# A decoder layer on one core: another order of the steps, the end in two halves, and the cross stage's maxima added by VectorE

## The reference

```python
x = layernorm(x + attention(x))               # 16 heads of 8, causal, rope before the second projection
x = layernorm(x + cross_attention(x, ctx))    # 16 heads of 8, 154 context tokens, rope, biases
x = layernorm(x + ffn(x))

def ffn(x):                                   # x: 1024 tokens of 128
    probs = softmax(x @ wg.T)                 # 8 experts
    topk_w, topk_idx = top_k(probs, 2)        # renormalised to sum 1
    expert_w = one_hot(topk_idx) summed with topk_w
    h1 = einsum('th,eih->tei', x, w1)         # inner width 256 per expert
    h3 = einsum('th,eih->tei', x, w3)
    y = einsum('tei,ehi->teh', silu(h1) * h3, w2)
    return einsum('te,teh->th', expert_w, y)
```

## Time and profile before

| | |
|---|---|
| median of three runs | 267.58 us (266.43 to 268.08) |
| profiled execution | 266.47 us |
| span of that execution, first to last instruction | 264.7 us |
| mean granted TensorE clock | 0.987 |
| busy share: PE, PEld, DVE, ACT, POOL | 88%, 60%, 69%, 59%, 36% |

### The profile page before, as it was taken

The page is one execution under the profiler, slowest core; times in us unless marked ns, Lnnn a source line. Parts: engine busy times, 40 slices in busy tenths (PEclk is TensorE's granted clock), DMA queues, the critical chain, the costliest instruction groups (busy, mean ns, idle before and its releaser), DMA issues. The chain is left out here.

```text
span 264.7 us, 4496 instructions
## 1 busy us (share of the span) xinstructions
PE 233.1 (88%) x1385; PEld 160.1 (60%) x1385; DVE 184.0 (69%) x614; ACT 156.9 (59%) x311; POOL 95.4 (36%) x153
## 2 busy tenths in 40 slices
PE   7677999989998989999998966979799999999960
PEld 3254775666674656666654344554389788897850
DVE  6558878884999886765955569993177873679543
ACT  1669576786789956875887642547466755221300
POOL 9983292174413355241744511065000102711001
PEclk9979999999999999999999999999999999999997
DMA  6970000001000400000031200001411121101001
GB/s 240 340 264 1 2 0 1 2 29 53 2 0 0 158 2 1 4 0 0 5 115 41 83 0 1 0 30 52 120 30 32 31 62 40 50 22 40 1 1 42
DMA packets 10552, 12.57 MB, mean 47 GB/s; under 512 B 1184, under 2 KB 7712, under 8 KB 10400
## 3 DMA queue, kind: packets, MB, share of 16 engines
q1 hardware_dynamic: 9440, 10.43, 12.1%
q0 software_dynamic: 512, 1.05, 1.3%
q10 hardware_dynamic: 576, 0.79, 0.8%
HBM read 9.25 MB, written 3.01 MB: 46 GB/s over the span
## 5 line engine op out<-in xcount | busy, mean ns | idle before, releaser
L1450 DVE CUSTOM_DVE_ANT_0 junk<-psA,c 128x128 bf16<-128x128 f32 (+3 forms) x128 | 56.0, 487 | 14.2 <-PE psA L969 13.6
L1244 ACT ACTIVATE prob<-psB 128x512 f32<-128x512 f32 (+1 forms) x88 | 47.1, 559 | 13.2 <-PE psB L998 12.5
L969 PE MATMUL psA<-kst,qa 128*128 128x512 f32 (+1 forms) x88 | 37.7, 441 | 3.7 <-DVE negm L1450 1.8
L998 PE MATMUL psB<-qb,kst 128*128 128x512 f32 (+3 forms) x128 | 38.6, 346 | 2.5 <-ACT prob L1244 1.0
L998 PEld LDWEIGHTS psB<-qb,kst 128*128 128x128 f32 x128 | 22.8, 188 | 17.8 <-issue 8.5
L1455 DVE TENSOR_REDUCE negm<-psA 128x3 f32<-128x462 f32 (+1 forms) x48 | 26.3, 578 | 10.1 <-PE psA L969 10.0
L1244 ACT ACTIVATE prob_more<-psB 128x512 f32<-128x512 f32 (+1 forms) x48 | 24.5, 528 | 10.8 <-PE psB L998 10.2
L821 POOL TENSOR_SCALAR_AFFINE_SELECT prob<-prob 128x256 f32<-128x256 f32 x32 | 13.1, 408 | 45.6 <-ACT prob_more L1244 45.5
L969 PEld LDWEIGHTS psA<-kst,qa 128*128 128x128 f32 x88 | 16.9, 194 | 11.8 <-issue 6.9
L853 POOL TENSOR_SCALAR mv<-mv 128x4 f32<-128x4 f32 x6 | 1.4, 228 | 61.2 <-DVE mv L1487 61.0
L1286 ACT ACTIVATE silu<-psA 128x512 f32<-128x512 f32 x16 | 9.6, 598 | 22.5 <-PE psA L875 21.2
(11 more groups left out here) (180 smaller groups left out, 536.0 us busy)
## 6 DMA issues: line engine op xcount, KB each, us to landing
c<-w_dram SPq DMA_DIRECT2D x8, 256.0 KB, 2.7
w<-w_dram SPq DMA_DIRECT2D x1, 1024.0 KB, 4.7
xs_dram<-kst SPq DMA_DIRECT2D x1, 960.0 KB, 7.1
ys_dram<-ys SPq DMA_DIRECT2D x7, 128.0 KB, 1.8
rest<-xs_dram SPq DMA_DIRECT2D x3, 256.0 KB, 3.4
c<-c_dram SPq DMA_DIRECT2D x1, 666.0 KB, 8.6
xT<-xt_dram SPq DMA_DIRECT2D x2, 256.0 KB, 4.8
x_tok<-x_dram SPq DMA_DIRECT2D x1, 512.0 KB, 10.4
```

The costliest lines, as they stand in the source:

```text
L969: last = nc.tensor.matmul(ps[:, c:c + heads * width].rearrange("p (n w) -> p n w", n=heads), qa[:, u % SLOTS, 128 * i:128 * i + 128], keys ...
L998: last = nc.tensor.matmul(ps[:, c:c + S - 128 * kt], keys, qb[:, u % 2, 128 * kt:S], start=m == 0, stop=m == len(blocks) - 1, skip_group_c ...
L1244: nc.scalar.activation(dst, psB[n % SIZE["B"]][:, 0:cols], ACT.Exp, scale=SCALE).then_inc(b_done[n % SIZE["B"]], 1)
L1450: last = nc.vector.tensor_tensor_reduce(out=junk[:, p, cols], in0=psA[p][:, cols], in1=c32[:, C_MASK + S - width:C_MASK + S], scale=-1.0, ...
```

## The change

Three things. First, a table `EARLY` of 65 steps with numbers from -103 to 90; `schedule()` adds them to the priority among stages that could begin at the same moment, so a positive one is taken sooner. Second, in the cross stage MT has no identity product: TensorE only transposes the maxima into the bank, and VectorE adds bank and `qa` into `qb`, where ScalarE copied; the slot of `qa` is then free when VectorE is done. Third, the last expert's F2 and the last LN, LNX and OUT become halves of two tiles of 128 tokens: FL (8 matmuls, two gated sums), LE (statistics on VectorE, the root with ScalarE's Sqrt and VectorE's reciprocal, normalisation) and OE (a transfer of 128 KB). RO calls Sqrt once behind the last silu and tanh. Left out of the diff: FL's name in the ring J, the new tiles and semaphores, EPS as a constant, and LN and LNX without their case for batch 1.

```diff
@@ -177,7 +177,7 @@
     row = lambda u: (u // NG // B, u // NG % B)
-    q_slot = lambda u: [(("MT", (u - SLOTS,)), 0)] if u >= SLOTS else []
+    q_slot = lambda u: [(("MT", (u - SLOTS,)), unit(u - SLOTS)[0])] if u >= SLOTS else []
 
@@ -241,7 +241,7 @@
         add("MP", (u,), [("POOL", 0.55) if st == 0 else ("DVE", 0.4)], [("A", (u, len(fills) - 1))] + ([(("MT", (u - 2,)), 0)] if u >= 2 else []))
-        add("MT", (u,), [("PE", 0.67), ("ACT", 0.5)], [("MP", (u,))],
+        add("MT", (u,), [("PE", 0.67), ("ACT", 0.5)] if st == 0 else [("PE", 0.45), ("DVE", 0.69)], [("MP", (u,))],
             [(1, (("B", (u - 2, len(b_fills(u - 2)) - 1)), 0))] if u >= 2 else [])
@@ -319,12 +319,17 @@
             [(1, ("F1", (f,)))] + ([(1, (("F2", (f // 2 - 2,)), 0))] if f >= 4 else []))
-        if f % 2:
+        if f % 2 and f < FT - 1:
             add("F2", (f // 2,), [("PE", 1.76), ("DVE", 0.95)], [("F3", (f,)), ("W2", ())], [(1, ("GATE", (1,)))])
-    for b in range(B):
-        add("LN", (2, b), [("DVE", 1.2), ("POOL", 1.3)], [("F2", (E - 1,)) if b else ("YC", ())])
-        add("LNX", (2, b), [("DVE", 1.05)], [("LN", (2, b))])
-        add("OUT", (b,), [("SP", 0.6)], [("LNX", (2, b))], after=2.0)
+    add("LN", (2, 0), [("DVE", 1.2), ("POOL", 1.3)], [("YC", ())])
+    add("LNX", (2, 0), [("DVE", 1.05)], [("LN", (2, 0))])
+    add("OUT", (), [("SP", 0.6)], [("LNX", (2, 0))], after=2.0)
+
+    add("RO", (), [("ACT", 1.5)], [(("F1", (FT - 1,)), 1), (("R1", (NT - 1,)), 1)])
+    for h in range(2):
+        add("FL", (h,), [("PE", 0.95), ("DVE", 0.55)], [("F3", (FT - 2,)), ("F3", (FT - 1,)), ("W2", ()), ("F2", (E - 2,))])
+        add("LE", (h,), [("DVE", 0.65), ("ACT", 0.25), ("DVE", 0.75)], [("FL", (h,)), ("RO", ())])
+        add("OE", (h,), [("SP", 0.6)], [("LE", (h,))], after=2.0)
     return table
@@ -378,7 +383,7 @@
                 begin = max([begin] + [ends[k] + LATENCY[engine[k]] for k in held])
-            score = (begin, -way[key])
+            score = (begin, -way[key] - early(item))
             if best is None or score < best[0]:
@@ -401,6 +406,24 @@
 
+EARLY = {
+    ('A', 3): 90, ('A', 4): 8, ('A', 5): 26, ('A', 6): -19, ('B', 0): -30, ('B', 1): 8, ('B', 11): 2, ('B', 15): -22,
+    ('B', 2): 20, ('B', 5): 22, ('B', 6): 34, ('B', 8): -6, ('B', 9): 5, ('F1', 0): -16, ('F1', 15): 33, ('F1', 2): 3,
+    ('F1', 9): 26, ('F2', 0): -43, ('F2', 2): -12, ('F2', 3): -6, ('F2', 4): -32, ('F3', 10): -22, ('F3', 12): 48,
+    ('F3', 13): 8, ('H', 1, 'q'): -57, ('LG', 1): -38, ('MP', 12): 4, ('MP', 14): 10, ('MP', 9): 38, ('MT', 1): -20,
+    ('MT', 2): -55, ('MT', 4): -23, ('ONT', 0, 1): 9, ('OP', 0, 0): -54, ('OP', 1, 1): -42, ('OT', 2): -4, ('PV', 1): -35,
+    ('PV', 10): -27, ('PV', 2): -15, ('PV', 7): 28, ('PV', 8): -38, ('R1', 0): -66, ('R1', 10): -3, ('R1', 11): -26,
+    ('R1', 2): -14, ('R1', 9): -17, ('R2', 10): 37, ('R2', 4): -12, ('R3', 0): 2, ('R3', 14): -55, ('R3', 3): -18,
+    ('R3', 4): 6, ('R3', 7): -10, ('R3', 8): 3, ('SC', 0): -10, ('SK', 0, 1): -14, ('SK', 0, 2): -25, ('SQ', 0, 0, 3): -14,
+    ('SQ', 0, 1, 0): -27, ('SQ', 1, 0, 0): -15, ('SQ', 1, 0, 2): 31, ('U', 0, 'v'): -18, ('U', 1, 'v'): -27, ('XS', 2): -103,
+    ('XS', 3): -27,
+}
+
+
+def early(item):
+    kind, args = item
+    return EARLY.get((kind,) + (args[:1] if kind in ("A", "B", "PV", "MK") else args), 0.0)
+
 SEND = 1.2
...
@@ -735,10 +765,14 @@
                 elif kind == "OUT":
-                    b, = args
-                    sp.wait_ge(s_x, 4 + b + 1)
-                    sp.dma_start(out_d[b].rearrange("(i p) d -> p i d", p=128), x_tok[:, b, :, :]).then_inc(s_out, 16)
-            sp.wait_ge(s_out, 16 * B)
+                    sp.wait_ge(s_x, 5)
+                    sp.dma_start(out_d[0].rearrange("(i p) d -> p i d", p=128), x_tok[:, 0, :, :]).then_inc(s_out, 16)
+                elif kind == "OE":
+                    h, = args
+                    sp.wait_ge(s_xe, h + 1)
+                    sp.dma_start(out_d[1].rearrange("(i p) d -> p i d", p=128)[:, 2 * h:2 * h + 2, :],
+                                 x_tok[:, 1, 2 * h:2 * h + 2, :]).then_inc(s_out, 16)
+            sp.wait_ge(s_out, 16 * 3)
 
@@ -977,10 +1011,11 @@
                     pe.wait_ge(s_frr, NG + 1)
-                    nc.tensor.matmul(ps[:, :], fr_id[:, :], qa[:, u % SLOTS, :], start=True, stop=False, skip_group_check=True)
+                    if st == 0:
+                        nc.tensor.matmul(ps[:, :], fr_id[:, :], qa[:, u % SLOTS, :], start=True, stop=False, skip_group_check=True)
                     for i in range(QT):
-                        last = nc.tensor.matmul(ps[:, 128 * i:128 * i + 128], mpad[:, u % 2, i, :], fr_id[:, :], start=False,
-                                                stop=i == QT - 1, skip_group_check=True)
+                        last = nc.tensor.matmul(ps[:, 128 * i:128 * i + 128], mpad[:, u % 2, i, :], fr_id[:, :], start=st == 1,
+                                                stop=st == 1 or i == QT - 1, skip_group_check=True)
                     last.then_inc(j_full, 1)
@@ -1092,6 +1127,15 @@
                                                     w2[:, 128 * f:128 * f + 128], start=f == 2 * e, stop=f == 2 * e + 1)
+                    last.then_inc(j_full, 1)
+                elif kind == "FL":
+                    h, = args
+                    ps = bank(JOB[item])
+                    fill_done(pe, "B", [("F3", (FT - 2,)), ("F3", (FT - 1,))])
+                    for i in (2 * h, 2 * h + 1):
+                        for f in (FT - 2, FT - 1):
+                            last = nc.tensor.matmul(ps[:, 128 * i:128 * i + 128], hid[:, f % 4, 128 * i:128 * i + 128],
+                                                    w2[:, 128 * f:128 * f + 128], start=f == FT - 2, stop=f == FT - 1)
                     last.then_inc(j_full, 1)
@@ -1194,8 +1238,10 @@
                     u = unit_of(st, b, g)
-                    if u >= SLOTS:
+                    if u >= SLOTS and unit(u - SLOTS)[0] == 0:
                         job_filled(act, ("MT", (u - SLOTS,)))
+                    elif u >= SLOTS:
+                        job_done(act, "MT", u - SLOTS)
                     free(JOB[item], nc.scalar.activation(qa[:, u % SLOTS, :], ps[:, :], ACT.Copy))
@@ -1284,6 +1330,14 @@
                     nc.scalar.activation(silu[:, f % 2, :], psA[a % SIZE["A"]][:, :], ACT.Silu).then_inc(a_done[a % SIZE["A"]], 1)
+                elif kind == "RO":
+
+                    nc.scalar.activation(root[:, :], c32[:, C_ONE + 1:C_ONE + 2], ACT.Sqrt)
+                elif kind == "LE":
+                    h, = args
+                    act.wait_ge(s_mve, h + 1)
+                    nc.scalar.activation(rstd_e[:, 2 * h:2 * h + 2], mv_e[:, 2 * h:2 * h + 2, 1], ACT.Sqrt,
+                                         bias=c32[:, C_ONE + 1:C_ONE + 2]).then_inc(s_sqe, 1)
                 elif kind == "XS":
@@ -1392,6 +1446,12 @@
                                             ALU.subtract).then_inc(s_mp, 1)
+                elif kind == "MT":
+
+                    u, = args
+                    ps = bank(JOB[item])
+                    dve.wait_ge(s_b, FILL["B"]["B", (u - 2, len(b_fills(u - 2)) - 1)] + 1)
+                    free(JOB[item], nc.vector.tensor_tensor(qb[:, u % 2, :], ps[:, :], qa[:, u % SLOTS, :].bitcast(FP32), ALU.add))
                 elif kind == "VH":
@@ -1609,6 +1669,31 @@
                     nc.vector.tensor_tensor(hid[:, f % 4, :], psB[h % SIZE["B"]][:, :], silu[:, f % 2, :], ALU.mult).then_inc(b_done[h % SIZE["B"]], 1)
+                elif kind == "FL":
+                    h, = args
+                    ps = bank(JOB[item])
+                    for i in (2 * h, 2 * h + 1):
+                        ins = nc.vector.scalar_tensor_tensor(out=z2[:, i, :], in0=ps[:, 128 * i:128 * i + 128], scalar=gw[:, 0, i, E - 1:E],
+                                                             in1=z2[:, i, :], op0=ALU.mult, op1=ALU.add)
+                    free(JOB[item], ins)
+                    job_free(dve, JOB[item])
+                elif kind == "LE":
+                    h, = args
+                    tiles = (2 * h, 2 * h + 1)
+                    if item not in marked:
+                        marked.append(item)
+                        for i in tiles:
+                            last = nc.vector.bn_stats(stats_e[:, i, :], z2[:, i, :])
+                        link(last)
+                        for i in tiles:
+                            last = nc.vector.bn_aggr(mv_e[:, i, :], stats_e[:, i, :])
+                        last.then_inc(s_mve, 1)
+                        continue
+                    dve.wait_ge(s_sqe, h + 1)
+                    link(nc.vector.reciprocal(rstd_e[:, 2 * h:2 * h + 2], rstd_e[:, 2 * h:2 * h + 2]))
+                    for i in tiles:
+                        last = nc.vector.tensor_scalar(x_tok[:, 1, i, :], z2[:, i, :], mv_e[:, i, 0:1], rstd_e[:, i:i + 1], ALU.subtract, ALU.mult)
```

(17 more changed lines are left out.)

## The result

The changed kernel takes 259.58 us, median of four runs (257.58 to 262.91), beside 267.25 us for the kernel before: ratio 0.969, 95% interval [0.962, 0.976], 8.3 us less. Run twice more, on other chips, the changed kernel gave 0.970 [0.965, 0.976] and 0.972 [0.965, 0.979]. The prediction had the direction and missed the size by a factor of two: 4.0 us said, 8.3 us measured. The median of 259.58 us stands at the outermost edge of its range, 259.5 to 267.8.

The account below looks back on a forecast made before the run. TensorE was taken as the bound late and where cross units begin, with idle holes elsewhere and a bare chain at the end. Terms -1.8 - 0.3 - 1.9 = -4.0 us took 267.58 to 263.6 us, range 259.5 to 267.8.

Parts of the forecast that it names:

- The halves: End of the kernel behind the last matmul: two overlapping halves and a smaller last transfer save 1.8 us, bounds -1.2 to -2.3.
- The sum: Cross units 8 to 15: VectorE's sum replaces TensorE's identity product and ScalarE's copy; -0.3 us, bounds -1.8 and +2.0.
- (b): Rival: VectorE becomes the bound in 164 to 181 us, costing +2.0 there; 266.4 us in all, chance 0.13.
- The order: Biases recover TensorE idle time in 15 to 40 and 140 to 190 us: -1.9 us, bounds +2 and -4.5.
- one named collision: Batch 1's four normalisations (LNX) take 3.05 us under GpSimd's weight splits (L827); moving them clear gives 1.9 us.
- The holes: TensorE's idle time in 140 to 190 us was to fall from 9.15 us to 5 to 8.
- The hole behind 150 us: TensorE runs out of batch 0 while batch 1's chain to its cross units is unfinished; if it stays, the prediction is wrong.
- (a): Rival: the order brings nothing, some idle time goes and other comes; 265.5 us in all, chance 0.17.
- (c): Rival: silu and tanh alternate, 2.6 us of table loads each time; three make 271.3 us; chance 0.08 with other losses.
- (d): Rival: VectorE takes both gated sums before any statistics, the end gains only 1.0 us; 264.4 us, within main case's 0.62.

Follow-up runs that it names:

- new_first_old_late: Kernel before's instructions, self attention and batch 0's way to its first cross query in the changed kernel's order, the rest in the old order: 0.9954 of before.
- fill_before: Kernel before plus 12 and 6 matmuls whose results nobody reads, ahead of unit 13's maxima and XT(1,0): 0.996 of before.
- the splices: Kernel before's instructions, one part of every queue in the changed kernel's order: self attention new 0.9954 of before, everything behind it new 0.9818.

## Why the prediction was right in direction and wrong in size

- **The halves, -1.8 us: right.** 1.75 us on the timeline, 1.5 and 1.9 us in the runs. The chain is 3.74 us long (3.5 to 3.7 said), the transfer's share 0.42 (0.3 said); the root took 0.29 us, not 0.20, with no effect on the first half and 0.1 us on the second.
- **The sum, -0.3 us: right within its bounds, for a partly wrong reason.** Its price, 0.69 us also under GpSimd's splits, was right, but the 0.9 us for units 8 to 11 never showed: the whole sum is worth 0 in the new order and +1.2 us in the old one. TensorE's waits for the maxima in the third stretch are 2.2 us before and after, so VectorE did not become the bound there as rival (b) had it.
- **The order, -1.9 us: the step that failed.** I took "a fifth of the reachable idle time", set to the size of one named collision (1.9 us is a fifth of the 9.15 us of 140 to 190; of the 12.6 us that I had named, with the 3.4 of 15 to 40, it is less). The runs give 6.5 us [5.2, 7.7] for the same instructions in the new order, beyond the bound of -4.5. Two errors stand behind it. First, I let one collision carry the whole estimate; it gave 1.0 us of its 1.9 and was one piece of many. Second, I called reachable only what lay in the two stretches with visible holes, and wrote of 217 to 254 that "only less TensorE work helps". The three shares of 1.3, 2.3 and 2.4 us say otherwise. Between 40 and 140 us the kernel before had 4.8 us of idle time and the changed one 3.0; ahead of an F2 stood the wait of 0.54 us, which the new order doesn't have, and in other runs of the old order waits of up to 1.4 us (new_first_old_late, fill_before). The 1.29 us ahead of the last F2, which stand in the earlier trace rows, the new order left as they were (1.30); moving F3(15) takes them.
- **The holes**: TensorE's idle time in 140 to 190 is 7.1 us, inside the 5 to 8 predicted, but with a granted clock of 0.86 in that stretch. The hole behind 150 us shrank, from 8.1 to 6.3 us between batch 1's last CQ product and the first tanh, and most of it is still there.
- **The rivals**: (a) is excluded by the order's interval; (b) by the waits above; (c) did not come, since tanh and silu don't alternate and one load stands between them; (d) did not come, since the statistics stand between the gated sums.

Left open: what makes up the 1.3 us of self attention, and which of the 65 biases count. Nor do the runs tell why the sum costs 1 us in the old order; its profile ran 13.8 us of its third stretch at half clock, against 7.2 with the halves alone.

## What to carry to other kernels

A reordering's worth is bounded by all idle time of the bounding engine, gaps of 0.3 to 1.3 us in "full" stretches included, not by the holes that one can name: here it recovered 6.5 us, of which the order of cross attention, where the named hole is, held about a third. In these traces part of what it recovered are waits for a VectorE that is late for other reasons, and what covers them is more steps between F3 and the F2 that needs its `hid`. Test a new order with the old instructions in it, and each new instruction in the old order, since a planner that answers to a cost hides which of the two moved the time (the same sum was +5.4, +1.2 and 0 us). And compare traces from event to event, after subtracting what ran at the lower clock; a lead of 4.1 us at one event was worth 1.3 us at the end, partly for that reason.

## What was not expected of the hardware

The granted clock falls inside a kernel whose TensorE is 88 to 91% busy. Stretches of 3 to 14 us at 0.50 (1.2 GHz) came between 152 and 194 us in all profiled executions but the first one of the kernel before, in some also at 81 to 89, 131 to 135 or 253 to 256 us, at places that change from one execution to the next. The executions of the kernel before beside the splices show the price: 268.7 and 269.3 us of span at a mean clock of 0.987, 270.5 and 271.0 at 0.964 and 0.965. Four of the changed kernel run from 255.5 us at 0.979 to 260.0 at 0.956. In each set of executions of the kernel before the lower clock goes with the longer span (correlations of -0.6 to -0.9), so much of what looks like scatter in these times is the clock.
